# Two attention and FFN layers on one core: the order of transposes, values, first FFN chunk and first scores where one group ends and the next begins

## The reference

```python
x = x + _L0_xattn_ref(_layernorm(x), ctx, ctx, ...)      # 16 heads of 16, no mask
x = x + _L0_ffn_ref(_layernorm(x), w_gate, w_up, w_down)  # blockwise FP4, silu(gate) * up, inner size 704
x = x + _L1_xattn_ref(_layernorm(x), ctx, ctx, mask, ...) # 16 heads of 64, masked
x = x + _L1_ffn_ref(_layernorm(x), w1, b1, w2, b2)        # inner size 1024
```

```python
h = jnp.einsum('bsd,df->bsf', x, w1) + b1
h = float2fix(h, MANT_BITS)                       # multiples of 2^-8
h = pwlin_gelu_basic(h, MANT_BITS, MANT_BITS)     # GELU, linear between 33 points
h = float2fix(h, MANT_BITS)
out = jnp.einsum('bsf,fd->bsd', h, w2) + b2
return float2fix(out, MANT_BITS)
```

## Time and profile before

| | us |
|---|---|
| median of 3 runs | 935.86 |
| lowest, highest | 935.5, 937.94 |
| the profiled execution | 935.95 |
| its span in the profile | 934.1 |
| TensorE busy | 899.9 (96%) |
| VectorE busy | 669.7 (72%) |
| ScalarE busy | 601.8 (64%) |
| GpSimd busy | 203.9 (22%) |

### The profile page before, as it was taken

The page is one execution under the profiler, slowest core; times in us unless marked ns, Lnnn a source line. Parts: engine busy times, 40 slices in busy tenths (PEclk is TensorE's granted clock), DMA queues, the critical chain, the costliest instruction groups (busy, mean ns, idle before and its releaser), DMA issues.

```text
span 934.1 us, 16212 instructions
## 1 busy us (share of the span) xinstructions
PE 899.9 (96%) x5610; PEld 603.8 (65%) x5610; DVE 669.7 (72%) x2179; ACT 601.8 (64%) x1671; POOL 203.9 (22%) x316
## 2 busy tenths in 40 slices
PE   5999999999999999999999999999999999999998
PEld 2555576667656567577675566666756655757686
DVE  5999883763889786475598978366478888837468
ACT  3788425972779644795369953499267984369735
POOL 3211002872000000476000000077400000028500
PEclk9999999999999999999999999999999999999999
DMA  9500000000000000000000010000000000000000
GB/s 298 204 1 2 29 0 24 2 1 1 1 1 25 1 28 24 1 2 2 1 0 8 18 29 1 24 1 2 1 0 1 19 7 1 1 0 2 2 1 23
DMA packets 14561, 18.35 MB, mean 20 GB/s; under 512 B 3089, under 2 KB 11665, under 8 KB 14481
## 3 DMA queue, kind: packets, MB, share of 16 engines
q1 hardware_dynamic: 12288, 15.40, 5.0%
q10 hardware_dynamic: 2064, 1.91, 0.7%
q0 software_dynamic: 128, 0.01, 0.0%
HBM read 15.21 MB, written 2.10 MB: 19 GB/s over the span
## 4 chain that ended last, share of the span: by engine, by line
PE 71%; DVE 15%; ACT 10%; issue 3%; POOL 1%; DVEq 0%; POOLq 0%
PE bank L1238 27%; PE bank L1253 9%; PE bank L1506 6%; PE bank L1592 6%; PE bank L1486 5%; PE bank L1344 4%; ACT ring L672 4%; PE bank L1401 3%; DVE row_max L1045 3%; PE bank L1378 3%; ACT ring L713 2%; PE bank L1461 1%; PE bank L1472 1%; ACT ring L557 1%; PE bank L1556 1%
## 5 line engine op out<-in xcount | busy, mean ns | idle before, releaser
L464 POOL TENSOR_TENSOR rstd<-var_eps,minus_half 128x2 f32<-128x2 f32 x32 | 23.4, 734 | 539.7 <-DVE var_eps L883 539.7
L557 ACT ACTIVATE ring<-bank 128x512 f32<-128x512 f32 x224 | 123.4, 611 | 17.5 <-PE bank L1253 17.5
L482 POOL TENSOR_TENSOR ring<-ring,row_inv 128x256 f32<-128x256 f32 x192 | 112.1, 612 | 95.4 <-DVE row_inv L1140 95.4
L1253 PE MATMUL bank<-ident_s,ring 128*128 128x128 f32 x768 | 105.1, 279 | 4.9 <-POOL ring L482 2.3
L1253 PEld LDWEIGHTS bank<-ident_s,ring 128*128 128x128 f32 x768 | 82.6, 141 | 39.5 <-issue 17.4
L713 ACT ACTIVATE ring<-ring,row_max 128x256 f32<-128x256 f32 x192 | 95.0, 496 | 17.3 <-DVE row_max L1133 17.3
L672 ACT ACTIVATE ring<-bank,row_max 128x256 f32<-128x256 f32 x192 | 88.2, 494 | 4.0 <-DVE row_max L1045 4.0
L1133 DVE CUSTOM_DVE_ANT_0 ring<-bank,maskbias 128x256 f32<-128x256 f32 x192 | 70.7, 420 | 23.4 <-issue 23.4
L1045 DVE TENSOR_REDUCE row_max<-bank 128x2 f32<-128x512 f32 x128 | 79.3, 681 | 5.7 <-PE bank L1378 4.9
L1238 PE MATMUL bank<-wgu_s,act_s 128*128 128x352 f32 x256 | 78.4, 459 | 0.0
L1238 PE MATMUL bank<-ctxT_s,wk_s 128*128 128x512 f32 x160 | 75.6, 596 | 0.7 <-DVE v L1031 0.7
(11 more groups left out here) (190 smaller groups left out, 1748.0 us busy)
## 6 DMA issues: line engine op xcount, KB each, us to landing
x_s<-x SPq DMA_DIRECT2D x4, 512.0 KB, 4.0
ctxT_s<-ctxT SPq DMA_DIRECT2D x4, 512.0 KB, 4.6
w_s<-w SPq DMA_DIRECT2D x2, 1024.0 KB, 16.2
out<-act_s SPq DMA_DIRECT2D x16, 128.0 KB, 1.7
wk_s<-wk SPq DMA_DIRECT2D x1, 1024.0 KB, 13.3
wv_s<-wv SPq DMA_DIRECT2D x1, 1024.0 KB, 14.6
wq_s<-wq SPq DMA_DIRECT2D x1, 1024.0 KB, 16.2
wo_s<-wo SPq DMA_DIRECT2D x1, 1024.0 KB, 16.5
```

What stands on the lines that cost most here:

```text
L482: ins = pool.tensor_tensor(probs1[i % PRING1][:, a, :], probs1[i % PRING1][:, a, :], row_inv[:, i, a:a + 1].to_broadcast([P, SEQ]), ALU.mult)
L557: act.activation(probsT[u % TRING][:, :, :].rearrange("p a q -> p (a q)"), psum(at, key)[:], ACT.Copy).then_inc(drain(at, key), 1)
L1253: ins = pe.transpose(psum(at, key)[:, c * SEQ + a * P:c * SEQ + (a + 1) * P], tile[:, a, c * P:(c + 1) * P], ident_s[:])
```

## The change

Three places are rewritten; no work is added or dropped.

In `last_hidden` TensorE no longer does all four values first. It does the first half of the `xT3` transposes, both halves of `xT0`, values 0 and 1, then waits for the second half of xn, does its transposes, value 2, waits for both `xT3` halves to be read out, and does FFN chunk 0. Value 3 follows behind chunk 0. ScalarE reads the transposes out in the new order, and VectorE reads out value 3 within the first step of the GELU. Last, the scores of the next group stand behind five chunks of the second product, not six.

```diff
--- before.py
+++ after.py
@@ -49,6 +49,7 @@
 KEYS_AHEAD = 1
 AHEAD, BEHIND = 1, 1
 FIRST_SCORES_AFTER = 4
+VALUES_AHEAD = 3
 HALF_QUERIES = 2
 WARM_UP = 4
 POOL_PIECES = range(1, 5)
@@ -634,9 +635,9 @@
 
             def last_layer(at, g):
 
-                for h in range(HALVES):
-                    evacuate_xT(at, 3, h, xnT)
+                evacuate_xT(at, 3, 0, xnT)
                 layer0_inputs(at)
+                evacuate_xT(at, 3, 1, xnT)
                 for m in range(FC1 + AHEAD):
                     if m < FC1:
                         if m >= GELUS:
@@ -927,6 +928,8 @@
                     if m < FC1:
                         dve.tensor_scalar(bits(buf[:, 1, :]), bits(buf[:, 0, :]), LINE_BITS, LINE_BASE_BITS, ALU.bitwise_and,
                                           ALU.bitwise_or).then_inc(g_knot, 1)
+                        if m == 0:
+                            layer0_values(at, range(VALUES_AHEAD, TILES))
                     if u >= 0:
                         dve.wait_ge(g_line, line + 2)
                         dve.tensor_tensor(prev[:, 1, :], prev[:, 1, :], prev[:, 3, :], ALU.add).then_inc(g_line, 1)
@@ -1024,9 +1027,9 @@
                 dve.wait_ge(o_round, g * TILES + t + 1)
                 dve.tensor_tensor(res_b[:, t, :], ffn_out[:, t, :], res_b[:, t, :], ALU.add).then_inc(out_ready, 1)
 
-            def layer0_values(at):
-
-                for t in range(TILES):
+            def layer0_values(at, tiles):
+
+                for t in tiles:
                     dve.wait_ge(*is_filled(at, ("v0", t)))
                     dve.tensor_tensor(v0[:, t, :, 0:3:2, :], psum(at, ("v0", t))[:, 0:DM].rearrange("p (i n d) -> p i n d", n=2, d=DK0),
                                       bv0_s[:].rearrange("p (i n d) -> p i n d", n=2, d=DK0), ALU.add).then_inc(drain(at, ("v0", t)), 1)
@@ -1062,7 +1065,7 @@
                     if r == 0:
                         if g is None:
                             dve.wait_ge(values_loaded, 16 * 2)
-                            layer0_values(at)
+                            layer0_values(at, range(TILES))
                     for i in round_units0(r):
                         if i == 2 and g is not None:
                             output_bias(at)
@@ -1217,7 +1220,7 @@
             quantized_norm(opening_pass, 0)
             for g in range(GROUPS - 1):
                 fp4_and_layer1(middles[g], g, g + 1)
-                layer0_values(crossings[g])
+                layer0_values(crossings[g], range(VALUES_AHEAD))
                 gelu(crossings[g], g)
                 layer0_heads(crossings[g], g * UNITS + UNITS, g)
                 quantized_norm(crossings[g], g + 1)
@@ -1321,16 +1324,25 @@
                     closing_output(at, g, m, 1)
 
             def last_hidden(at, ln):
-                for h in range(HALVES):
-                    pe.wait_ge(xn_ready, ln * TILES + 2 * h + 2)
-                    transpose_xn(at, 3, h, xn)
+                pe.wait_ge(xn_ready, ln * TILES + 2)
+                transpose_xn(at, 3, 0, xn)
 
                 for h in range(HALVES):
                     transpose_xn(at, 0, h, xn0)
+
+                for t in range(2):
+                    layer0_values(at, t)
+                pe.wait_ge(xn_ready, ln * TILES + TILES)
+                transpose_xn(at, 3, 1, xn)
+                for t in range(2, VALUES_AHEAD):
+                    layer0_values(at, t)
                 for h in range(HALVES):
                     pe.wait_ge(*is_drained(at, ("xT3", h)))
                 for m in range(FC1):
                     product(at, ("f", m), psum(at, ("f", m))[:], [(w1_s[:, c, m * P:(m + 1) * P], xnT[:, c, :]) for c in range(KC)])
+                    if m == 0:
+                        for t in range(VALUES_AHEAD, TILES):
+                            layer0_values(at, t)
 
             def last_out(at, g, chunks):
 
@@ -1614,13 +1626,11 @@
             layer0_heads(opening_pass, 0, True)
             for g in range(GROUPS - 1):
                 fp4_and_layer1(middles[g], g, crossings[g])
-                for t in range(TILES):
-                    layer0_values(crossings[g], t)
                 last_hidden(crossings[g], g * 4 + 4)
                 layer0_queries(crossings[g])
-                last_out(crossings[g], g, range(6))
+                last_out(crossings[g], g, range(5))
                 layer0_scores(crossings[g], 0)
-                last_out(crossings[g], g, range(6, FC1))
+                last_out(crossings[g], g, range(5, FC1))
                 for m in range(KEYS_AHEAD):
                     layer1_key(crossings[g], m)
                 layer0_heads(crossings[g], g + 1, False)
```

## The result

| | us |
|---|---|
| kernel before, median of 20 runs | 937.08 (935.5 to 938.69) |
| changed kernel, median of 20 runs | 940.43 (938.9 to 942.09) |
| ratio | 1.0036, 95% interval 1.0028 to 1.0044 |
| profiled execution, span in the profile | 937.3 (before 934.1) |

The change makes the kernel 3.4 us slower; 3.6 us were forecast. The page of the changed kernel shows how little of this an overview tells. Busy times (first line, by engine) are those of before to within 1.3 us, since no work was added; TensorE's, VectorE's and ScalarE's differ by 0.8 us at most. What differs is who stands on the chain that ended last: VectorE with 20% of the span and TensorE with 64% (second line), before 15% and 71% (third line, from the page of the kernel before).

The account below looks back on a forecast made before the run. TensorE is busy almost throughout, and VectorE's GELU pace sets ScalarE's query read-out. Three crossings of -0.3 and +1.49 us add 3.6 us to 935.95, giving 939.5 us, likeliest range 938.5 to 940.2, wider range 937.3 to 940.6.

Parts of the forecast that it names:

- The bound: Over the GELU, TensorE and VectorE are full and ScalarE follows VectorE; the second query's read-out hangs on VectorE's pace.
- Part one: New TensorE order ahead of the FFN: gains 0.3 us a crossing, bounds 0.08 to 0.43.
- Part two: Scores behind five chunks wait 1.5 us for the second query's read-out, with lag 0.35: costs 1.49 us a crossing.
- The sum: Three crossings, each -0.3 and +1.49 us, make 3 x 1.19 = 3.6 us slower, 939.5 us.
- the likeliest case: The scores' wait is paid in full in each crossing: 939.5 us, own range 938.5 to 940.2, chance 0.81.
- (A): Scores in the crossings do not wait, leaving only the gain ahead of the FFN: 935.0 us, chance 0.07.
- (B): The scores' wait is there but up to 1.19 us a crossing is taken back behind the key product: 936.0, chance 0.10.
- (C): The new wait ahead of the crossings' scores drops TensorE's clock to 1.2 GHz: about 958 us, chance 0.02.

Follow-up runs that it names:

- all values first: Part one alone, with the fourth value ahead of the first FFN chunk again: 935.52 us, ratio 0.9982.
- ordered waits: Changed kernel with the wait for the second query's bank put last ahead of the first scores, double waits left out: 938.89 us, ratio 1.0015.
- earlier queries: Changed kernel with ScalarE reading out each of the two query chunks one FFN chunk sooner: 936.07 us, ratio 0.9988.
- the kernels that moved the key's read-out: ScalarE's read-out of the first key product moved behind the exponentials of units 2 and 3: on the changed kernel ratio 0.9997, on part one alone 0.9945.
- the key's read-out on part one: Part one alone, with ScalarE's read-out of the first key product moved behind the exponentials of units 2 and 3: 932.5 us, ratio 0.9945.
- part one alone: Changed kernel with the first scores behind six output chunks again, keeping only the new order ahead of the FFN: 935.91 us, ratio 0.9985.
- all three edits: Part one alone plus the key's read-out behind the exponentials of units 2 and 3 and the ordered waits: 930.68 us, ratio 0.9936.
- part two alone: Kernel before with only the first scores moved behind five output chunks: 942.51 us, ratio 1.0051.
- the scores behind seven chunks: Changed kernel with the first scores behind seven output chunks, not five: 935.0 us, ratio 0.9971.
- the kernel before with and without ordered waits: Kernel before with only the waits ahead of the first scores reordered, second query's bank last: 936.4 us against 937.01 without, ratio 0.9993.

## Why the prediction was right

- **The bound.** VectorE's GELU stretch paced ScalarE, and so the queries' read-out, and TensorE's moves did not shift it: confirmed by the chain, and by part one and part two adding up (-0.38 and +1.50 are +1.12; together +1.10).
- **Part one.** A gain of 0.3 us was forecast from bounds of 0.08 to 0.43; it is 0.38. Two errors nearly cancel in the changed kernel. TensorE went on 0.06 us behind the normalisation (226.40 + 0.73 = 227.13 to 227.19), where I had put 0.14, and the third value hid the read-out of the last transposes, so the first chunk is at 4.56 us, not 4.65. But this chunk takes 1.80 us up to the fourth value (228.57 to 230.37), not the 1.725 that I took as the mean over ten products; so the second chunk is at 7.22 us, where the prediction's sum gives 7.24. What was off is the other side of the difference: I had put the second chunk of the kernel before at 231.755, with the same mean, and it starts at 231.83, with the weight load shown below, so 7.61 us behind the crossing's start and not 7.54. The second chunk's read-out moved by 0.38. That the first chunk's 1.2 us would not help was right, as the kernel with all values first shows.

```profile
231.83 0.19 PEld L1238 LDWEIGHTS bank<-act_s,w_s 128*128 128x128 f32 x1 [0.24 <-issue]
```

- **Part two.** The wait of 1.5 us is 1.42 us, and the lag behind the query's read-out 0.35 us, the value taken from the opening; the short lag of 0.14 would have given 2.9 us in all. That further waits behind the blocking one make the lag long is shown by the kernel with ordered waits, where it falls to 0.14 us. The page Perfetto Trace Analysis of the Trainium skill, section Identifying Dependency Chains, allows for extra semaphore instructions ahead of one that waits on several engines; it gives no time for them, and the 0.35 us here fit it.
- **The sum.** 3 x 1.19 = 3.6 us were forecast and 3.3 to 3.4 came: 3 x 1.11 in the crossings, 3.4 in the lowest and in the median times. The term that was off is part one's gain, by 0.08 us a crossing. The starting point was off by more: the 20 runs put the kernel before at 937.08, not at 935.86 as the first three did, though one of those three was at 937.94. The forecast of 939.5 is therefore 0.9 us under the median of 940.43, and this lies above the 940.2 that I gave as the likeliest case's own upper end; the wider range to 940.6, made for the noise of a median, holds it by 0.2 us. The difference between the two kernels is right to 0.3 us.
- **The rivals.** (A) needed the second query to be ready 1.5 us sooner; the kernel with earlier queries does just that, and gives -1.15 us in the medians, where (A) had said -0.9. (B) did not happen: the loss is there whole from crossing to crossing, and the kernels that moved the key's read-out show that gains of 1.2 us pass through too. Small gains pass less well: of the 0.8 us of the ordered waits the lowest time shows 0.55. (C) did not happen in the crossings: the granted clock of all three is 1.00 in the changed kernel, and its slowest executions are no farther from its fastest (3.2 us) than those of the kernel before (3.2 us). But the clock does fall in some executions, in the opening.

## What to carry to other kernels

Before work is moved ahead in one engine's queue, ask when its inputs come out of the other engines' queues, and what sets their pace. Here the scores were moved ahead, to a point where the query that they need was not yet read out. ScalarE's read-out hung on VectorE's pace, and the wait was paid in full because the whole queue stood behind it. An earlier start is worth something only if the reader of its result is free: scores 1.7 us earlier bought nothing, while the order of two read-outs on ScalarE was worth 1.25 us a crossing. Where several conditions stand ahead of one instruction, the one that comes last should be waited for last.

## What the hardware showed that was not expected

**The clock in the opening.** In the profile of the key's read-out on part one, the granted clock falls to its lower level of 1.2 GHz behind the opening's wait of 1.84 us, and once more near 49 us, behind a wait of 1.45 us for VectorE. Both times TensorE had worked at a granted clock of 1.00 (2.4 GHz) for about 1.5 us since the wait (from 23.73 to 25.2, from 47.59 to 49.1). Both waits stand in the other profiles with the opening's 1.84 us too, without a fall. The windows of that kernel (stretch, length, busy time of each engine, granted clock, DMA):

```profile
24.80:26.50 1.70, 1.70 (x9) 1.39 (x6) 1.56 (x3) 1.29 (x4) 0.78 (x1) 0.62 1.03 412
26.50:28.00 1.50, 1.50 (x5) 1.16 (x4) 1.26 (x3) 1.50 (x9) 1.50 (x1) 0.50 1.02 377
28.00:30.30 2.30, 2.21 (x9) 1.55 (x7) 0.90 (x3) 1.49 (x8) 0.07 (x1) 0.87 1.11 360
...
48.90:51.70 2.80, 2.80 (x21) 2.04 (x21) 2.73 (x7) 0.71 (x2) 0.04 (x1) 0.54 0.00 0
```

Its timeline has the price: the four values of the opening take 5.41 us, 3.72 in the changed kernel.

```profile
24.81 5.41 PE L1241 MATMUL bank<-wv_s,ctxT_s 128*128 128x256 f32 x16
```

```profile
24.12 3.72 PE L1241 MATMUL bank<-wv_s,ctxT_s 128*128 128x256 f32 x16
```

The same work from the opening products to the first crossing takes 2.15 us longer in this profile than in the others (220.80 us, below).

**What spreads the executions.** The executions of one kernel lie up to 3 us apart, and the profiles show two things that shift them. One is this fall of the clock: in the 20 runs of the changed kernel the mean granted clock is 0.998 for the five at 941.1 to 941.44 and 0.996 for the four at 941.95 to 942.09, and 0.999 to 1.000 for the eleven below. But it does not part those eleven, of which seven lie at 938.9 to 939.29 and four at 940.19 to 940.5; in part one alone the four fastest (934.58 to 934.97) have 0.999 and the next three (935.81 to 936.25) 1.000. A step of this size, 1.2 us, is found between the profiles in the opening's first work on TensorE, four products on zeros (`WARM_UP`). They start at 6.78 or 6.79 us in every profile and take from 5.22 to 6.43 us. In the kernel with all three edits, and in the one with the key's read-out on part one:

```profile
6.79 5.26 PE L1608 MATMUL bank<-v 128*128 128x512 f32 x8 [6.79 <-POOL two L455]
```

```profile
6.78 6.05 PE L1611 MATMUL bank<-v 128*128 128x512 f32 x8 [6.78 <-POOL two L455]
```

Their matmuls start 0.85 us apart at first and 0.43 later, while the granted clock reads 1.00 throughout; what differs is how many keep the long distance (in part one alone it ends near 10 us, in part two alone behind 12). Everything behind them is shifted: the first crossing's start, less the time of these products, is 218.62 to 218.68 us in the eight profiles with the opening's wait of 1.84 us and no fall of the clock, 218.42 to 218.45 in the three with 1.63 us, and 220.80 in the one with the fall. Why the opening products change their pace sooner or later is not shown here.

The wait of 1.84 us is there in every execution, so it does not decide alone over the fall. But in the three kernels with ordered waits none of 27 executions has a mean clock of 0.998 or less, while 57 of the 147 with the longer wait do: nine of the 20 of the changed kernel, 24 of the 66 of the kernel before that ran beside the other kernels, but none of the six with the scores behind seven chunks. In the only pair that differs in nothing else and ran together, the kernel before with and without ordered waits, it is none of eleven against three of 15, which alone would not settle it. That the shorter wait is the cause rests on these counts; what else must come together for the clock to fall stays open. The page TensorE: Matmul & The Clock Gate of the Trainium skill, section A second HAM failure mode: psum-queue depth-cycling, tells of a bf16 kernel in which frequent short idle times between groups of matmuls make the clock go up and down. This kernel is float32 and its waits in the opening are single ones, so its two falls are like that case only in part. The waits of 1.42 and 1.20 us in the crossings, with TensorE busy all around, had no such effect in any profile here.

**The lag of a release.** TensorE starts 0.14 us behind ScalarE's end (257.42 to 257.56 with ordered waits) when the wait that blocks is the last of its instruction, and 0.35 us behind it (256.54 to 256.89 in the changed kernel) when four further waits stand behind. Behind VectorE's end it starts after 0.06 us (227.13 to 227.19 in the changed kernel), though one further wait, for the bank of the transposes, stands behind that one in the code; why this release is the shortest is not shown.
